# Small constants in tiles of their own, and the transposed expert weights declared last

## The reference

```
n = layernorm(x)                                     # x: 256 x 1024
feat = concat(n[src], n[dst])                        # per edge, 2048 wide
e = relu(feat @ W + b)                               # W_hh for 128 edges, W_oo for the next 640, W_ho for the rest
logit = e @ W_a + b_a;  alpha = softmax of logit over the edges with the same dst
z = segment_sum(alpha * n[src], dst)
x = x + relu(concat(n, z) @ W_node + b_node)         # W_hn for the first 64 nodes, W_on for the others
y = layernorm(x)
sim = (y @ hasher_w.T) @ keys.T;  the 4 best of 256 experts, w = softmax of their sim
out = sum over the 4 of  w_k * (silu(y @ values_down[k]) @ values_up[k])
x = x + (y + scale * out)
```

## Time and profile before

| | |
|---|---|
| median of three runs | 786.03 us |
| all runs | 786.44, 786.03, 785.1 us |
| the profiled execution | 786.44 us, with a span of 784.7 us |
| mean granted PE clock in it | 0.97 of full speed |
| instructions | 9683, of them 3305 matmuls |

### The profile page before, as it was taken

The page is one execution under the profiler, slowest core; times in us unless marked ns, Lnnn a source line. Parts: engine busy times, 40 slices in busy tenths (PEclk is TensorE's granted clock), DMA queues, the critical chain, the costliest instruction groups (busy, mean ns, idle before and its releaser), DMA issues.

```text
span 784.7 us, 9683 instructions
## 1 busy us (share of the span) xinstructions
PE 732.9 (93%) x3305; PEld 573.5 (73%) x3305; DVE 519.3 (66%) x833; ACT 352.8 (45%) x391; POOL 191.2 (24%) x333
## 2 busy tenths in 40 slices
PE   3999999988979998779999999999999999999998
PEld 3777767776656566548877788888888888888886
DVE  6897696677999999936489545445554544554543
ACT  3845799545534441113443443433443433444330
POOL 7203668798898404000000000000000000000000
PEclk9999999998989998769999999999999999999999
DMA  8784223350020013204823654566444466545421
GB/s 315 284 319 172 108 107 109 115 206 1 1 108 2 1 64 117 98 1 160 269 108 109 225 183 145 194 214 214 151 170 161 159 214 214 189 142 184 151 83 54
DMA packets 50059, 114.22 MB, mean 146 GB/s; under 512 B 2245, under 2 KB 35397, under 8 KB 44906
## 3 DMA queue, kind: packets, MB, share of 16 engines
q1 hardware_dynamic: 49418, 112.95, 40.5%
q0 software_dynamic: 160, 0.66, 0.2%
q10 hardware_dynamic: 448, 0.20, 0.1%
HBM read 112.74 MB, written 1.05 MB: 145 GB/s over the span
## 4 chain that ended last, share of the span: by engine, by line
PE 62%; POOL 14%; DVE 9%; issue 8%; ACT 5%; DVEq 1%; ACTq 0%; POOLq 0%
PE ps L1202 18%; PE ps L1204 18%; PE ps L1203 18%; POOL peak L493 5%; POOL pen L498 4%; POOL oh_src L495 4%; PE ps L1172 2%; DVE wlo L738 2%; DVE oh_dst L1031 2%; ACT chunk_col L594 1%; PE ps L1485 1%; ACT chunk_gap L589 1%; PE ps L1518 1%; PE ps L1193 1%; ACT whi L537 1%
## 5 line engine op out<-in xcount | busy, mean ns | idle before, releaser
L738 DVE TENSOR_TENSOR wlo<-raw,whi 128x2048 fp32r<-128x2048 f32 x104 | 235.8, 2290 | 72.6 <-ACT whi L537 70.9
L537 ACT ACTIVATE whi<-raw 128x2048 fp32r<-128x2048 f32 x104 | 196.1, 1911 | 101.1 <-PE ps L1204 94.9
L1202 PE MATMUL ps<-whi,nT_hi 128*128 128x512 f32 x424 | 173.6, 410 | 3.5 <-DVE wlo L738 2.3
L1204 PE MATMUL ps<-wlo,nT_hi 128*128 128x512 f32 x424 | 169.8, 400 | 0.0
L1203 PE MATMUL ps<-whi,nT_lo 128*128 128x512 f32 x424 | 169.4, 400 | 0.0
L928 DVE SCALAR_TENSOR_TENSOR ps<-ps,xt 128x1024 f32<-128x1024 f32 x80 | 97.7, 1222 | 5.5 <-PE ps L1226 5.0
L1202 PEld LDWEIGHTS ps<-whi,nT_hi 128*128 128x128 f32 x424 | 80.8, 191 | 24.0 <-DVE wlo L738 2.7
L1136 DVE TENSOR_TENSOR gw<-act_g,route 128x512 f32<-128x512 f32 x32 | 20.7, 689 | 114.1 <-ACT act_g L701 114.0
L1204 PEld LDWEIGHTS ps<-wlo,nT_hi 128*128 128x128 f32 x424 | 80.8, 191 | 19.8
L1203 PEld LDWEIGHTS ps<-whi,nT_lo 128*128 128x128 f32 x424 | 81.1, 191 | 18.1
L1202 PE MATMUL ps<-whi,gT_hi 128*128 128x512 f32 x240 | 93.8, 391 | 0.0
(11 more groups left out here) (236 smaller groups left out, 869.1 us busy)
## 6 DMA issues: line engine op xcount, KB each, us to landing
raw<-n_L_ffn_values_down_dram SPq DMA_DIRECT2D x16, 2048.0 KB, 8.3
raw<-in_L_ffn_values_up_dram SPq DMA_DIRECT2D x16, 2048.0 KB, 7.4
raw<-in_L_gnn_W_hh_dram SPq DMA_DIRECT2D x8, 1024.0 KB, 8.8
raw<-in_L_gnn_W_oo_dram SPq DMA_DIRECT2D x8, 1024.0 KB, 6.4
raw<-in_L_gnn_W_ho_dram SPq DMA_DIRECT2D x8, 1024.0 KB, 4.8
raw<-in_L_gnn_W_hn_dram SPq DMA_DIRECT2D x8, 1024.0 KB, 5.1
raw<-in_L_gnn_W_on_dram SPq DMA_DIRECT2D x8, 1024.0 KB, 4.8
xt<-in_x_dram SPq DMA_DIRECT2D x4, 512.0 KB, 5.5
```

The costliest lines, as they stand in the source:

```text
L537: nc.scalar.activation(half(whi, s, j, down), half(raw, s, j, down), ACT.Copy)\
L738: nc.vector.tensor_tensor(half(wlo, s, j, down), half(raw, s, j, down), half(whi, s, j, down).bitcast(F32), ALU.subtract)\
L1202: nc.tensor.matmul(o, a_hi, b_hi, start=start, stop=False)
L1204: return nc.tensor.matmul(o, a_hi, b_lo, start=False, stop=stop)
```

## The change

The tile `small` is replaced by eight tiles, each of which takes 32 bytes. Six of them stand where `small` stood or close by (`node`, `block_pos`, `rel_neg`, `spare`, `row_no`, and `sel_ones` behind `sel`), and `scale_b` and `ba_b` stand behind `bucket_first`. The tiles `gT_hi` and `gT_lo` are declared behind `gw` instead of ahead of `top`. Each engine has the same instructions with the same shapes in the same order; only addresses differ.

```
-        small = sb("small", [P, 48])
-        node, block_pos, rel_neg, spare, row_no, scale_b, ba_b = (
-            small[:, a:b] for a, b in ((0, 2), (2, 6), (6, 7), (7, 8), (8, 9), (9, 10), (10, 11)))
-        sel_ones = small[0:5, 11:12]
+        node = sb("node", [P, 2])
+        block_pos = sb("block_pos", [P, 4])
+        rel_neg = sb("rel_neg", [P, 1])
+        spare = sb("spare", [P, 1])
+        row_no = sb("row_no", [P, 1])
         ident = sb("ident", [P, P])
         ident16 = sb("ident16", [P, P], F16)
         ones16 = sb("ones16", [P, P], F16)
         below16 = sb("below16", [P, P], F16)
         sel = sb("sel", [5, 5, P], F32R)
+        sel_ones = sb("sel_ones", [5, 1])
...
         bucket_first = sb("bucket_first", [P, NBK])
+        scale_b = sb("scale_b", [P, 1])
+        ba_b = sb("ba_b", [P, 1])
...
         hT_sb = sb("hT_sb", [2 * PD, N])
-        gT_hi = sb("gT_hi", [P, BLOCKS, N], F32R)
-        gT_lo = sb("gT_lo", [P, BLOCKS, N], F32R)
         top = sb("top", [P, NT, 8])
...
         gw = sb("gw", [P, NT, GX * PD])
+        gT_hi = sb("gT_hi", [P, BLOCKS, N], F32R)
+        gT_lo = sb("gT_lo", [P, BLOCKS, N], F32R)
```

## The result

| | |
|---|---|
| median before | 785.43 us (6 runs, 783.58 to 786.44) |
| median after | 791.57 us (6 runs, 789.7 to 791.93 and one of 906.7) |
| ratio | 1.0074, 95% interval 1.0056 to 1.0091, which is +5.8 us (4.4 to 7.1) |
| profiled execution after | 790.35 us, span 788.6 us (before: 786.44 and 784.7) |

The run of 906.7 us had a mean granted clock of 0.745 against 0.967 to 0.976 in the others; it is left out of the ratio, and the median of the other five is 791.3 us.

What follows compares the result with a forecast made beforehand. The prediction took PE's matmul distances in the expert-group loop as the bound. Its four terms, 0 + 0 + 0 + 0, left 786.4 us against the profiled execution, 786.0 against the median; the range was 784.6 to 795.6 us.

Steps and rivals of the forecast that it cites:

- What bounds the kernel: Loop over expert groups, 430 to 762 us: PE busy throughout, only matmul start-to-start distance counts; ACT and DVE wait.
- Part 1, gT: 720 matmuls of `up` with gT stationary, remainder 0 to 32: 0 us taken, bounds -9.6 and +9.6 us.
- The first rival: gT's load in `up` becomes visible from remainder 32: up to +9.6 us, 795.6 us; chance 0.31.
- middle case: In `up`, the 13.3 ns not streaming grow by half: 720 x 6.7 ns = +4.8 us, 790.8 us.
- The sensor: gT's load row in `up`: above 188 ns if the load costs, setting the matmul distance from about 324 ns.
- The rule of the Trainium skill: SBUF lines of 16 bytes, accesses pay under two hits a line; gT at remainder 32 gets four: 0 us.
- Part 2, ident and sel: Constants ident, ident16, ones16, below16, sel from remainder 0 to 32, 172 transposes with ident: 0, bound 0.5 us either way.
- Part 3, everything by 64 bytes: Tiles moved by 64 bytes, and act_g, gw, route by 8128: remainder by 64 unchanged, so 0 us.
- The announced proof: For the load rival: gT distances over 227 ns while `gT_last` and nT_hi matmuls keep theirs.
- Part 4, constants: Short constants in tiles of their own, read as one number per partition and instruction: 0 us.
- The clock rival: Half-clock stretch before 356 us falls elsewhere: 784.4 or 787.6 us; chance 0.17 together with other early effects.

Runs made afterwards that it cites:

- the kernel put right by 256 bytes: Changed kernel plus unused tiles, 192 bytes behind ba_b and 224 ahead of gT_hi, float32r operands behind ba_b at old remainders by 256: ratio 0.9993 (0.9984 to 1.0002).

## Why the prediction was wrong, step by step

- **What bounds the kernel**: right. The PE-bound loop carried most of the loss, 5.0 of the 6.7 us of the sum, and no other engine's busy time changed by more than 0.2 us.
- **Part 1, gT**: the step that failed. The place, the count of 720 and the price's upper bound (13.4 ns) were right; the value chosen between the ends was 0 (720 x 0 = 0 us), and 6.9 ns a matmul was measured, +5.0 us. It was taken from L1246 and `gw`, and both rows were about something else: their moving operands are not float32r streams of 512 columns that a float32r load runs beside. What the step compared was each tile's own remainder by 64; what the runs showed is that the start of gT relative to the moving tile counts, by 256 bytes.
- **The first rival** came near in its number (790.8 us in its middle case, 791.57 measured), and its place, `up`, was right. Its mechanism was not: it blamed a start at remainder 32, and gT at remainder 0 by 64 but 64 bytes off costs 6.7 ns a matmul as well. That the two numbers are close is luck.
- **The sensor** in part 1 and in the first rival failed too. The cost was expected to show in the load's row, from 324 ns on. It shows in no load's row: the loads of gT read 188 or 189 ns in the changed kernel, and 187 to 191 ns in every other run. Only the distance in ns between the matmuls has it.
- **The rule of the Trainium skill** that stood beside it, the 16-byte lines of "SBUF — State Buffer", section "Door 1: The DMA port swizzle", gave a sum of 0 for a contiguous run at any start. The measurement differs: with both gT tiles shifted, contiguous runs cost 4.9 to 8.9 ns a matmul at every pair of offsets tried, and the measurement decides. What was found here hangs on two operands that are read at once, and the rule as it was used looks at one.
- **Part 2, ident and sel**: right in its value. The transposes kept their 0.79 us, though by their addresses `gw` and `ident` lie 96 bytes apart by 256 before and 192 after, never 0, so this doesn't show that transposes are free of the cost. And the kernel put right by 256 bytes measures the same as before with both still shifted.
- **Part 3, everything by 64 bytes**: wrong, by 1.7 us in the sum. It was put at 0 since the remainder by 64 stays. The remainder by 256 did not, and zT, gT_last and tab_dst lost 4 to 7 ns each. The announced proof, that `gT_last` would keep its time, was refuted by the same thing.
- **Part 4, constants**: right, nothing.
- **The clock rival**: not the cause, since the loop runs at a granted clock of 1.00 in both kernels. As noise it is likely real: the profiled execution of before has a mean clock of 0.970, that of the changed kernel 0.976, and the former comes 2.1 us later to `zT`. No run shows that the clock alone makes these 2.1 us.
- **What the trace of before could have told**: the 2.4 ns between even and odd chunks of `down`. There the byte distance between stationary and moving operand alternates between 0 and 128, and the difference could have raised the question. It wasn't seen, because only absolute remainders were compared. It would not have given the rule, since `down` costs nothing at 64 and 192.

## What to carry to other kernels

When two float32r operands are streamed at once, compare the starts of the stationary and the moving tile with each other: with both operands contiguous, a distance that is no multiple of 256 bytes cost 2 to 4% of each 512-column matmul in `up`, with zT, with gT_last and in the edge weights, though not in the window loop, nor in `down` at 64 and 192. A small tile declared in between shifts everything behind it. The load's own row stayed at 188 ns while the matmuls beside it got 7 ns longer, so take the distance from start to start. And give the moving operand as one run, if an engine copies it anyway: that was worth more than the whole change.

## What the runs showed of the hardware that was not expected

- In `up` the relative address counts, not the absolute one. With all tiles 64 bytes further on the time was 784.6 us; with gT alone 64 bytes further on, 789.28 us.
- In `up` every distance tried but a multiple of 256 bytes costs, and 4 and 16 bytes cost more (8.9 ns in the mean) than 128 (5.5 ns). Whether a multiple of 256 is always free was shown only for the tiles of this kernel.
- Some products don't react. The one-hot products of the window loop (`tab_src` with `ring`) take 232 to 233 ns at distance 0 and 231 to 232 at 64; why they neither reach 226.7 ns nor react was not tried. In `down`, with its broken runs, 64 and 192 bytes cost nothing against 0 (236.4 and 236.6 ns), and 128 costs 2.4 ns. The group transposes take 109 ns a matmul at both of their distances, 96 and 192; at 0 they were never run.
- Sixteen runs of 128 bytes instead of one run of 2 KB cost about 11 ns of a 512-column matmul, 237.8 against 226.7 ns, while ACT and DVE read such runs at full speed (1912 and 2288 ns for 2048 elements, as before).
